# Rounding weights in a fused attention and FFN block: the last of four passes becomes an accumulating DMA, and GpSimd takes every first difference

## The reference, cut to what matters

```python
def _quantized_matmul(x, w, scale):
    wq = w.astype(jnp.float8_e4m3fn).astype(x.dtype)
    y = jnp.einsum('bsi,io->bso', x, wq)
    return y * scale
gate = jax.nn.silu(_quantized_matmul(x, gate_w, gate_scale))
up = _quantized_matmul(x, up_w, up_scale)
fuse = gate * up
return _quantized_matmul(fuse, down_w, down_scale)
```

```python
def step(S, inp):                       # attention: one chunk of 16 tokens, 128 in all
    kh = jnp.einsum('bchd,bhde->bche', ki, S)
    ...
    S = S - jnp.einsum('bchd,bche->bhde', ki * ei[..., None], v_new)
```

## Time and profile before

| | |
|---|---|
| median of 3 runs | 890.64 us (889.45 to 890.83) |
| profiled execution, its own time | 887.37 us |
| its span in the trace | 885.6 us |
| TensorE busy | 793.8 us (90%) |
| VectorE busy | 676.8 us (76%) |
| ScalarE busy | 496.7 us (56%) |
| Pool busy | 480.5 us (54%) |
| mean granted TensorE clock | 0.953 |

### The profile page before, as it was taken

The page is one execution under the profiler, slowest core; times in us unless marked ns, Lnnn a source line. Parts: engine busy times, 40 slices in busy tenths (PEclk is TensorE's granted clock), DMA queues, the critical chain, the costliest instruction groups (busy, mean ns, idle before and its releaser), DMA issues.

```text
span 885.6 us, 22947 instructions
## 1 busy us (share of the span) xinstructions
PE 793.8 (90%) x8308; PEld 558.6 (63%) x8308; DVE 676.8 (76%) x2704; ACT 496.7 (56%) x1328; POOL 480.5 (54%) x848
## 2 busy tenths in 40 slices
PE   9867777688978999999999999999999999978896
PEld 4444444456566666667676676766676766766795
DVE  3688887788878787778787878778777878767444
ACT  2776675667657565655646475656565564633331
POOL 6355756565556656556465546565665646445300
PEclk9887798798989999999999999999999999979998
DMA  8012121211211001000100010000100010001000
GB/s 274 25 49 61 34 64 36 62 37 37 61 37 37 2 2 49 2 26 2 49 2 26 1 38 14 26 1 2 50 2 25 3 48 2 2 2 48 1 24 25
DMA packets 16721, 28.48 MB, mean 32 GB/s; under 512 B 3520, under 2 KB 3520, under 8 KB 16608
## 3 DMA queue, kind: packets, MB, share of 16 engines
q1 hardware_dynamic: 16608, 27.02, 9.9%
HBM read 22.82 MB, written 4.19 MB: 31 GB/s over the span
## 4 chain that ended last, share of the span: by engine, by line
PE 59%; DVE 17%; POOL 10%; ACT 7%; issue 6%; DMA 1%; SPq 1%; POOLq 0%; DVEq 0%; ACTq 0%
PE bank L630 17%; PE bank L426 15%; PE bank L663 8%; PE bank L606 4%; PE bank L581 4%; POOL rho L1180 3%; PE bank L440 3%; PE bank L558 2%; ACT BDk L893 2%; PE bank L567 2%; PE bank L589 2%; DVE work L1492 2%; DVE f L1574 1%; PE bank L454 1%; DVE work L1496 1%
## 5 line engine op out<-in xcount | busy, mean ns | idle before, releaser
L1180 POOL TENSOR_TENSOR rho<-sy,cst 128x2 f32<-128x2 f32 x128 | 89.5, 700 | 236.4 <-DVE sy L1465 236.4
L581 PEld LDWEIGHTS bank<-VX,BDkR 128*64 128x64 f32 x1024 | 45.1, 140 | 93.1 <-issue 53.1
L1508 DVE TENSOR_TENSOR SQ<-SQ,bank 128x128 f32<-128x128 f32 x128 | 36.6, 286 | 79.2 <-PE bank L581 78.0
L581 PE MATMUL bank<-VX,BDkR 128*64 128x64 f32 x1024 | 57.0, 233 | 40.4 <-DVE VX L1501 40.4
L948 ACT ACTIVATE qhR<-bank 128x64 f32<-128x64 f32 x128 | 28.2, 221 | 102.6 <-PE bank L589 102.0
L907 ACT ACTIVATE BDkR<-kR,cst 128x128 f32<-128x128 f32 x256 | 81.3, 397 | 0.0
L663 PE MATMUL bank<-DW,fh 128*128 128x512 f32 x188 | 80.4, 428 | 0.6 <-DVE fl L1581 0.6
L893 ACT ACTIVATE BDk<-bank 32x256 f32<-32x256 f32 x124 | 46.4, 374 | 53.8 <-DVE kR L1407 46.1
L663 PE MATMUL bank<-DW,fl 128*128 128x512 f32 x188 | 75.2, 400 | 0.0
L1487 DVE SCALAR_TENSOR_TENSOR work<-work,rho,rR 128x32 f32<-128x32 f32 x256 | 53.1, 248 | 25.9 <-POOL rho L1180 25.7
L558 PEld LDWEIGHTS bank<-SQ,BDk 128*64 128x64 f32 x1024 | 46.2, 142 | 38.5 <-issue 34.4
(11 more groups left out here) (168 smaller groups left out, 2149.4 us busy)
## 6 DMA issues: line engine op xcount, KB each, us to landing
xt<-in_x SPq DMA_DIRECT2D x16, 256.0 KB, 2.8
x<-in_x SPq DMA_DIRECT2D x16, 256.0 KB, 2.8
out<-x SPq DMA_DIRECT2D x16, 256.0 KB, 2.1
yb<-in_gate_w SPq DMA_DIRECT2D x12, 256.0 KB, 2.7
yb<-in_up_w SPq DMA_DIRECT2D x12, 256.0 KB, 2.7
yb<-in_down_w SPq DMA_DIRECT2D x12, 256.0 KB, 2.7
Wk<-in_wk SPq DMA_DIRECT2D x1, 1024.0 KB, 6.1
Wv<-in_wv SPq DMA_DIRECT2D x1, 1024.0 KB, 7.9
```

The costliest lines, as they stand in the source:

```text
L581: ins = mm(dS[p, e], bdkr[:, gh, j % 4, p], VX[:, e], start=True, stop=True, skip_group_check=True)
L1180: tt(dst, src, cst[:, C_NH:C_NH + n], ALU.pow).then_inc(*one)
L1508: tt(S, S, dS.rearrange("p (g e) -> p g e", e=DH), ALU.add).then_inc(*scan_v.one("S"))
```

## The change

What it does:

- `magic`'s second activation writes the magic number into the unit's place in `GW`, `UW` or `DW`, and no longer over `wmg`. So `exponent` of the next unit waits for `s_magic`.
- `shift` reads it there and takes the difference the other way round, weight less magic number. Pool does it for all 36 units. In the 26 chunks that `pool_free` names it stays where it was; for the other 10 it stands at the end of Pool's work for the chunk, behind the roots.
- `quantize` leaves VectorE. It becomes a DMA that Pool issues right behind `shift`, once `s_shift` is there: it reads `wst` and adds it onto the magic number in the weights' place.
- `s_quant` becomes two semaphores, one for each parity of u, that a DMA raises by 16 when it has landed. SP waits for it before it loads unit u + 2, and TensorE waits for both before the first use of the weights.

```diff
-                            sp.wait_ge(s_quant, u + 1)
+                            sp.wait_ge(s_quant[u % 2], 16 * (u // 2 + 1))
                             stage(u + 2)
...
                 if p == 0:
-                    pe.wait_ge(*quantized(r // 2, 8))
+                    pe.wait_ge(*quantized(12 * (r // 2) + 8, 0))
+                    pe.wait_ge(*quantized(12 * (r // 2) + 8, 1))
...
-                fn(wmg[:, :], wmg[:, :], ACT.Identity, bias=epses[:, 6:7]).then_inc(s_magic, 1)
+                fn(place(u), wmg[:, :], ACT.Identity, bias=epses[:, 6:7]).then_inc(s_magic, 1)
...
                 pool.wait_ge(s_magic, u + 1)
-                tt(wst[u % 2][:, :], wmg[:, :], wst[u % 2][:, :], ALU.subtract).then_inc(s_shift, 1)
+                tt(wst[u % 2][:, :], wst[u % 2][:, :], place(u).bitcast(F32), ALU.subtract).then_inc(s_shift, 1)
+
+            def quantize(u):
+
+                pool.wait_ge(s_shift, u + 1)
+                nc.gpsimd.dma_start(place(u).bitcast(F32), wst[u % 2][:, :], accum_op=ALU.add).then_inc(s_quant[u % 2], 16)
...
                             after_rows(NC * t + j)
                             shift(u)
+                            quantize(u)
...
                     if j == 7 and fin:
                         fin_ry(h - 2, 0)
                         fin_ry(h - 2, 1)
+                    if scan and not pool_free(t, j):
+                        for u in unit_before(t, j):
+                            after_rows(NC * t + j)
+                            shift(u)
+                            quantize(u)
...
                 dve.wait_ge(s_stage[u % 2], 16 * (u // 2 + 1))
                 if u:
-                    dve.wait_ge(s_quant, u)
+                    dve.wait_ge(s_magic, u)
...
-                    for u in unit_before(t, j):
-                        if not pool_free(t, j):
-                            shift(u)
-                        quantize(u)
                     for u in unit_at(t, j):
                         exponent(u)
```

More of the change, by code:

```diff
@@ L181, in build @@
         s_stage = [sem(f"s_stage{n}") for n in range(len(wst))]
-        s_exp, s_over, s_magic, s_shift, s_quant = (sem(n) for n in ("s_exp", "s_over", "s_magic", "s_shift", "s_quant"))
+        s_exp, s_over, s_magic, s_shift = (sem(n) for n in ("s_exp", "s_over", "s_magic", "s_shift"))
+        s_quant = [sem(f"s_quant{n}") for n in range(2)]
         s_mask = sem("s_mask")
@@ L316, in unit, with quantized, place @@
             return w, (n % 4 * 3 + third if w < 2 else 4 * third + n % 4) * D
-        def quantized(third, n):
-            return s_quant, 12 * third + n
+        def quantized(n, k):
+            return s_quant[k], 16 * ((n + 1 - k) // 2)
+        def place(u):
+            w, e = unit(u)
+            return (GW, UW, DW)[w][:, e:e + D]
         def unit_at(t, j):
@@ L390, in body @@
                     elif n == 3:
-                        sp.wait_ge(s_quant, UNITS)
+                        sp.wait_ge(s_magic, UNITS)
                     sp.dma_start(x1[n % 4][:, :], x_t[n]).then_inc(s_xr[n % 4], 16)
@@ L656, in ffn_down @@
                     if p == 0:
-                        pe.wait_ge(*quantized(r // 2, 12))
+                        pe.wait_ge(*quantized(12 * (r // 2) + 12, 0))
+                        pe.wait_ge(*quantized(12 * (r // 2) + 12, 1))
                     if r == 0 and p > 0:
@@ L1587, in fin_y @@
                 else:
-                    dve.wait_ge(s_quant, UNITS)
+                    dve.wait_ge(*quantized(UNITS, k))
                 if p == 0 and k == 0:
```

## The result

The changed kernel takes 906.9 us (median of four, 904.0 to 910.0) against 890.1 before: a ratio of 1.0191, interval 1.0171 to 1.0211, or 16.8 us slower. The forecast was slower by 7.3 us (898, range 883 to 912). The sign and the range held, and the measured loss is more than twice the forecast one.

The account below looks back on a forecast made before the run. In passes with units, the scan's latency and VectorE's stream were taken as the bound. Chunk terms summed to +8.8, less 1.5, so +7.3 us: 894.7 for the profiled execution, 898 by the median, range 883 to 912.

Parts of the forecast that it names:

- price g: Pool's time per DMA issue, taken as 1.2 us between bounds 0.33 and 2.7; the sum is zero at 0.77.
- the landing: Accumulating transfer's time until its data has landed, taken as 3.3 us, after which SP may load unit u + 2.
- Pool's late `rho`: Pool's added work delays rho, for which VectorE waits; 16.4 us was to be lost to a late Pool.
- the load waits' price of 0: Loads wait for the landing but stay hidden by about 1 us before exponent; cost 0 to 2, taken as 0.
- Kinds A and C: A: five chunks with Pool already last, +6.4 us; C: six where qR's pass follows shift, -1.4 us.
- Kind B: Ten chunks whose shift moves from VectorE to Pool, behind the root; about 2.6 us added in each, +10.0 in all.
- The 1.5: Taken off because a late rho falls where VectorE waits for TensorE's update anyway, as in pass 2, chunk 7.
- Rival 2: Slow landing, 5.3 us instead of 3.3: exponent's load late in some 20 of 34 chunks, +9 more, about 907; chance 0.12.
- L1487's wait: VectorE's wait for Pool's rho, forecast to rise from 8.6 us to some 30 or more.
- Kind D: Other 15 chunks, Pool slack 1.6 to 4.5 us: 0.69 gained in nine, six wait for TensorE next; -6.2.
- A second step: Input loads xt and x1 stand behind a pass's last unit on SP; the landing was to delay them by nothing, 0.
- The fast-form lock: VectorE two-port operations and GpSimd lock each other out; exponent holding the issue in eight Kind B chunks would add 3.4.

Follow-up runs that it names:

- e1: Changed kernel with a third staging buffer, so that no load waits for the previous landing of its own buffer; 902.97 us, ratio 1.0175 to the kernel before.
- a2: Changed kernel with the ten units of Kind B given back to VectorE, the other 26 still by transfer; 899.4 us, ratio 1.0100 to the kernel before.
- h2: Kernel before with only the five units in chunks where Pool already came last moved to the transfer; 892.5 us, ratio 1.0042.
- c3: Kernel before with only Kind D's 15 units moved to the transfer, the magic number in the weights' place; 889.8 us, ratio 1.0001.
- k2: Kernel before with only the eleven units of Kinds A and C moved to the transfer; 895.3 us, ratio 1.0060.
- a1: Changed kernel with SP issuing the next pass's xt and x1 before the load of a pass's last unit; 903.2 us, ratio 1.0152 to the kernel before.
- h1: Kernel before with only the six units in chunks where Pool also forms qR moved to the transfer; 887.9 us, ratio 0.9991.
- k1: Kernel before with only Kind B's ten units moved to the transfer; 896.5 us, ratio 1.0072.
- d1: Changed kernel with exponent written as an operation with two inputs instead of one; 912.5 us, ratio 1.0277 to the kernel before.
- a3: Changed kernel with the addition left out: SP copies the difference over the weights' place and Pool issues nothing; 878.1 us, ratio 0.9861 to the kernel before.
- a4: Changed kernel with Pool making the last addition itself instead of issuing a transfer; 908.1 us, ratio 1.0213 to the kernel before.

## Why the forecast had the direction and missed the size

**Right.** The price g = 1.2 (measured 1.2), the landing (3.4 for 3.3), Pool's late `rho` as the largest new wait, and the load waits' price of 0 (e1). Kinds A and C: forecast +5.0, measured +5.3 together. Kind B: forecast +10.0, and after less a2 measures 8.1 (7.5 by the medians), 6.4 alone. The 1.5 that the forecast takes off at pass 2, chunk 7, stands behind a transfer of Kind A; in h2 0.9 of that wait was used up. Rival 2's number, 907, was met by luck: the landing was 3.4, not 5.3, and the load waits cost nothing.

**Signs that did not come.** VectorE was to be some 31 us less busy and is 18.5 (676.8 to 658.3); 8.2 of the rest is `exponent`, held by Pool (23.5 us in all against 15.3). L1487's wait was to reach 30 or more and reached 22.7. `exponent` was to show no wait for its load and shows 4.2, one of the signs that the forecast named for being wrong.

**The step that failed** is Kind D, "the other 15 ... 9 x 0.69 = -6.2". Alone these chunks give +0.1 (-1.7 to +1.9), and joined to A and C they cost 3.6, give or take 4. This one term is 6.3 too low alone and 9.8 too low in company, and the whole sum is short by 9.7; the other errors cancel (A and C 0.3 too low, B 1.9 too high, and 1.5 taken off at the end that these figures don't show). The reading behind it was that a chunk gains what leaves VectorE's tail unless the next one already waits for TensorE. I had counted the waits of before, and not all of them: in that trace the next chunk waits for TensorE in nine of the fifteen and not in six. The three that I left out wait for 0.41, 0.55 and 0.64 us, which by my own rule makes the term -4.6. The larger part is that a gain makes new waits: c3's waits for the update went from 21 to 25 in number and from 20.6 to 26.5 us, 1.3 of it behind TensorE's full stream (pass 4, chunk 0) and 1.2 behind matmuls at the lower clock (pass 2, chunk 3). Also, the only Pool result that I followed was `rho`. `bt`, needed by VectorE in chunk 6, stands behind transfers too, and its wait rose from 3.8 to 8.4 (c3) and to 12.2 (after). It is not Kind D's alone: k2, without D, has 10.3.

**A second step** was "`xt` and `x1` stand behind the stage of a pass's last unit ... : 0". It held for before's timing and broke at pass 3. There one landing took 4.7, SP came to x1 only at 187.97, and the load took 4.5 beside two others, and ScalarE had it at 192.5. a1 prices this at 3.5 us, give or take 4. It is not added to the 9.8: a2 and k2 contain parts of it (L1574 waits 1.8 us in k2, 3.2 in a2, 5.5 in after).

**Where terms don't add.** A alone costs 3.7, not 6.4; B alone 6.4, not 8.1; and A, B, C and D alone sum to 9.4 where together they cost 17.0, more than the intervals allow (about 4 either way). My reading is that each kind alone finds slack downstream that soaks up part of it, and that in company this slack is used once. h2 shows it in one place (1.73 to 0.84); for the rest it is argued. The slope fits it: 0.63 us per us of Pool up to the change's load and 0.9 beyond it.

**The fast-form lock.** The forecast named it for Kind B, at +3.4, with `exponent` holding up Pool's issue. It came the other way round and elsewhere: Pool's issue and `qR` pass hold `exponent`, in the six chunks of Kind C, and alone they cost nothing (h1). In k1, Kind B alone, only one `exponent` of 36 is longer than 0.75. The Trainium skill (SBUF — State Buffer, Who interferes with whom) says that between a VectorE operation in a two-port mode and GpSimd, whoever issues first gets the shared ports for the whole instruction, and that a VectorE operation with two inputs contends with a GpSimd one that reads; the traces agree on both (1.79 for an `exponent` that began 0.09 behind Pool's pass; 2.04 for the two-input form at the same place of d1). That an issue by itself holds `exponent` is not shown: in k1, where a `rho` follows the issue, the one long `exponent` (1.40) stands beside Pool's `shift`.

**Open.** Whether Kind D costs beside A and C, or only fails to gain: the interval of the 3.6 reaches 0. Two things go with it in a2's trace: TensorE's mean granted clock over 28 to 309 us is 0.85 where k2 has 0.88, and VectorE's wait for the update is 27.9 us against 20.0. At pass 2, chunk 3, a2 loses 1.4 us where k2 loses none, and a2's twelve matmuls take 4.38 there and k2's 2.77. Whether the clock falls because the chunks are longer, or makes them longer, no run here separates, and each kernel has one trace.

## What to carry to other kernels

A transfer issued by GpSimd is not free work: here it held Pool for 1.28 us, as long as the addition that it replaced, so it pays only where Pool's whole stream has that slack, for each of its consumers and not just the most frequent one. When work leaves an engine that is bound by latency, don't book the gain per chunk from the waits of before; ask which wait the engine runs into once it arrives earlier, and try the subset that is thought to be free by itself. And before a pass is moved to another engine, look whether it has to be there: two converting copies replaced four passes and gave 37 us, where no placing of the old ones that rounds the weights as asked gave anything clear of noise (h1, 0.8 us).

## What the runs showed of the hardware

- A DMA issue on GpSimd is logged at 0.91 us for 256 KB accumulated and 0.87 for 512 bytes: nearly independent of size. The next instruction starts about 0.6 into it and is lengthened (1.27 to 1.58, 0.70 to 1.02). SP's issue of the plain copy in a3 took 0.47. The Trainium skill (DMA: Bandwidth & Descriptors, Specifications) puts the first byte from GpSimd at about 1 us. That is a latency, near the length of the issue here, and what Pool loses is more, 1.28.
- The accumulating transfer of 256 KB within the core's memory lands in 3.4 us (median; 3.3 to 5.0), 4.7 at the turn to pass 3. The plain copy between the same two places in a3 lands in 2.4 (2.3 to 4.5), and a plain transfer to memory outside takes 2.1.
- VectorE's `exponent`, 0.42 us alone, lasted up to 2.55 beside GpSimd's issue and pass, up to 1.50 beside GpSimd's passes alone (a4), and its two-input form up to 2.29. In the kernel before no `exponent` was above 0.43, but its two-input `quantize` of 0.68 lasted up to 1.75.
- Twelve matmuls of the projection (128x512 outputs) took 2.77 us where the granted clock was 1.00 (before), and 5.24 where it was 0.52 (after).
- VectorE's CAST from float32 to an 8-bit float, 128x512, takes 0.42 us, no more than a bitwise operation on the same tile.
